# A graph network's scatter sum with weights and stream exchanged in its second round

## The reference, cut to what matters

```python
row, col = edge_index            # = src, dst: 400000 edges, 12500 nodes, H = 64
for t in range(2):               # two rounds
    m_input = concatenate([x[col], x[row], edge_attr], axis=1)
    messages = m_input @ msg_W[t].T + msg_b[t]
    agg = segment_sum(messages, row, num_segments=12500)
    x = gru_cell(agg, x, ...)    # r, z = sigmoid(...), n = tanh(...), (1 - z) * n + z * x
```

## Time and profile before

| | us |
|---|---|
| median of 3 runs | 2404.67 |
| lowest, highest | 2390.03, 2408.36 |
| the profiled execution | 2394.16 |
| its span, first to last instruction | 2392.5 |
| first tile of round 2 to the end, about | 1568 to 2392 |

### The profile page before, as it was taken

How to read it: one execution, slowest core, us unless ns; L and a number is a source line. 1 busy time by engine, 2 the same in 40 slices (tenths; PEclk the granted TensorE clock), 3 DMA queues, 4 the chain that set the end, 5 groups by cost and what they waited for, 6 DMA issues and landing times. The chain is left out here.

```text
span 2392.5 us, 126600 instructions
## 1 busy us (share of the span) xinstructions
PE 1623.6 (68%) x47260; PEld 1526.9 (64%) x47260; DVE 2179.6 (91%) x3727; ACT 1963.7 (82%) x4428; POOL 616.3 (26%) x853
## 2 busy tenths in 40 slices
PE   0000000000139999999999999869999999999996
PEld 0000000000138899999999999868999999999996
DVE  7999999999269899999999999868999999999995
ACT  4777894553158899999999999868999999999996
POOL 1000000000643344554444544301121211112121
PEclk9999999999969999999999999989999999999998
DMA  6100001111427676666677676566777777777773
GB/s 118 28 0 0 0 0 48 35 22 34 113 57 239 211 227 226 227 229 223 231 224 231 226 229 227 167 200 218 236 239 231 237 241 232 235 239 234 234 237 113
DMA packets 175418, 400.70 MB, mean 167 GB/s; under 512 B 73071, under 2 KB 76789, under 8 KB 174855
## 3 DMA queue, kind: packets, MB, share of 16 engines
q1 hardware_dynamic: 116907, 204.17, 27.6%
q0 software_dynamic: 57296, 195.19, 24.7%
q10 hardware_dynamic: 1132, 0.27, 0.1%
HBM read 384.63 MB, written 14.57 MB: 167 GB/s over the span
## 5 line engine op out<-in xcount | busy, mean ns | idle before, releaser
L1202 ACT ACTIVATE rows<-ps_rows 128x512 f16<-128x512 f32 x2744 | 1454.6, 632 | 74.7 <-PE ps_rows L1124 55.5
L1141 PE MATMUL ps_sum<-rows,src 128*64 128x132 f16 (+1 forms) x21952 | 1151.5, 225 | 16.0 <-ACT rows L1202 11.0
L1141 PEld LDWEIGHTS ps_sum<-rows,src 128*64 128x64 f16 x21952 | 903.0, 142 | 29.0 <-ACT rows L1202 20.1
L1296 DVE TENSOR_TENSOR src<-iota_units,src_lane 128x2048 f16<-128x2048 f16 (+1 forms) x784 | 863.4, 1101 | 41.7 <-PE ps_sum L1141 41.6
L1124 PE MATMUL ps_rows<-rows_next,dst 128*64 128x128 f16 x10976 | 546.3, 220 | 37.9 <-DVE dst L1287 21.0
L1124 PE MATMUL ps_rows<-rows_now,dst 128*64 128x128 f16 x10976 | 545.4, 219 | 18.2 <-DVE dst L1287 7.3
L1287 DVE TENSOR_SCALAR dst<-lanes,lane_no 128x2048 f16<-128x2048 f16 (+1 forms) x784 | 533.0, 680 | 10.4 <-DMA lanes<-lanes_dram 10.1
L860 PE MATMUL ps_src<-ident,late 112*64 112x112 f32 x98 | 29.6, 333 | 624.6 <-DVE taken L930 613.0
L1124 PEld LDWEIGHTS ps_rows<-rows_next,dst 128*64 128x64 f16 x10976 | 411.3, 112 | 60.2 <-ACT rows L1202 21.5
L1124 PEld LDWEIGHTS ps_rows<-rows_now,dst 128*64 128x64 f16 x10976 | 412.0, 111 | 41.7 <-issue 12.7
L860 PEld LDWEIGHTS ps_src<-ident,late 112*64 112x64 f32 x98 | 14.1, 143 | 630.2 <-DVE taken L930 614.1
(11 more groups left out here) (188 smaller groups left out, 2039.0 us busy)
## 6 DMA issues: line engine op xcount, KB each, us to landing
lanes<-lanes_dram POOLq DMA_DIRECT2D x294, 512.0 KB, 4.9
lanes<-lanes_dram SPq DMA_DIRECT2D x294, 512.0 KB, 4.7
lanes<-lanes_dram POOLq DMA_DIRECT2D x98, 256.0 KB, 4.2
lanes<-lanes_dram SPq DMA_DIRECT2D x98, 256.0 KB, 4.2
rows_now<-parts_dram SPq DMA_DIRECT2D x112, 32.0 KB, 1.8
rows_next<-parts_dram SPq DMA_DIRECT2D x112, 32.0 KB, 3.8
parts_dram<-rows_now SPq DMA_DIRECT2D x1, 3136.0 KB, 16.2
sorted_dram<-planes SPq DMA_DIRECT2D x1, 3136.0 KB, 11.6
```

Of the source, the lines that this page charges most:

```text
L1141: last = nc.tensor.matmul(ps_sum[b][at, 0:width], hot[:, at], row, start=(j == 0), stop=(j == J - 1))
L1202: nc.scalar.activation(rows[:, (u + NU * b) % ring, 0:n, 0:2 * H], cut(ps_rows[(u + NU * b) % 4][:])[:, 0:n, :], ACT.Copy).then_inc(rows_r ...
L1296: nc.vector.tensor_tensor(src1[q][:, 0:len(units)], iota_units[:].rearrange("p (o l) k -> p o l k", o=1) .broadcast_to([P, len(units), P, ...
```

## The change

Only round 2 (`flipped = r > 0`) changes, and some preparation for it.

1. **Scatter.** Weights are now `row[:, at]`, 64 columns without gaps (once the high, once the low half), and the stream is `hot`, all 128 one-hot columns with their step of 8 bytes. The number of matmuls is the same. `ps_sum` then holds the sums already turned: high half in partitions 0 to 63, low half in 64 to 127.
2. **Taking the sums.** ScalarE's `take_sum` is gone. VectorE writes `scaled`, then low half / 2048 from PSUM into `sums` (64 x 128), then adds the high half from PSUM straight into `turned_now` (64 x 128). `joined` and the copy to `extras` are gone.
3. **Turning.** Only `copied` and `scaled` are turned: two matmuls for four; ScalarE copies 128 columns for 256.
4. **Extras.** Attribute sums and counts of all tiles are turned once, in tile 0, copied by ScalarE, stored to `extras_dram` by SyncE, and for every tile SyncE fetches 2 x 128 numbers into `turned_now`, behind a wait for the gates of two tiles before. SyncE does not go on to tile 1's lanes before the store has landed.
5. **Weights.** As the operands' places are exchanged in round 2, 13 transfers place the weights instead of 8.
6. **The end.** The last two tiles are turned ahead of the last scatter units instead of behind them.

```diff
-                sp.wait_ge(weights_in, 16 * 8)
+                sp.wait_ge(weights_in, 16 * 13)
...
+                    def fetch_extras(k, b):
+
+                        wait(sp, gates_ready, k - 1)
+                        plain(sp.dma_start(turned_now[b][H + 1:H + 3, P:2 * P],
+                                           extras_dram[bass.ds(k, 1), :, :].rearrange("o v p -> (o v) p"))).then_inc(extras_in[b], 16)
+
                     if not more:
                         def body(s, b, half):
                             fetch_lanes(sp, s)
+                            if not past(s, 1):
+                                sp.wait_ge(extras_kept, 1)
+                                sp.dma_start(extras_dram.rearrange("t v p -> t (v p)"), extras_across[0:NT, :]).then_inc(extras_out, 16)
+                                sp.wait_ge(extras_out, 16)
+                                sp.wait_ge(ones_in, 4)
+                            else:
+                                fetch_extras(s - 1, 1 - b)
...
                         if u == 0:
-                            wait(te, sum_ready, s - 1)
+                            wait(te, joined_ready if flipped else sum_ready, s - 1)
...
                             for at in HALVES:
-                                last = nc.tensor.matmul(ps_sum[b][at, 0:width], hot[:, at], row,
-                                                        start=(j == 0), stop=(j == J - 1))
+                                if flipped:
+                                    last = nc.tensor.matmul(ps_sum[b][at, 0:P], row[:, at], hot, start=(j == 0), stop=(j == J - 1))
+                                else:
+                                    last = nc.tensor.matmul(ps_sum[b][at, 0:width], hot[:, at], row,
+                                                            start=(j == 0), stop=(j == J - 1))
...
+                        if flipped:
+                            te.wait_ge(extras_kept, 1)
+                            nc.tensor.matmul(ps_T[high, 0:P], copied[b][:], ident[:], start=True, stop=True)
+                            nc.tensor.matmul(ps_T[low, 0:P], scaled[b][:], ident[:], start=True, stop=True).then_inc(turned, 1)
+                            return
...
+                        if flipped:
+                            te.wait_ge(joined_ready, k + 1)
+                            te.wait_ge(extras_in[b], 16 * half + 16)
...
+                    def turn_extras():
+                        for v in range(2):
+                            last = nc.tensor.transpose(ps_T[0:NT, v * P:(v + 1) * P], edge_sums[:, :, v], ident[:])
+                        last.then_inc(extras_turned, 1)
...
                     def take_sum(k, b):
+                        if flipped:
+                            return
...
+                        n = P if flipped else 2 * P
+                        nc.scalar.activation(turned_now[b][:, 0:n], ps_T[:, 0:n], ACT.Copy).then_inc(T_ready, 1)
...
+                        if flipped:
+                            wait(dve, turned, k - 1)
+                            plain(nc.vector.tensor_scalar(scaled[b][:], h[:, bass.ds(k, 1), 0:H].rearrange("p o f -> p (o f)"),
+                                                          both[:, 1:2], None, ALU.mult)).then_inc(scaled_ready, 1)
+                            dve.wait_ge(scattered, (k + 1) * NU)
+                            wait(dve, joined_ready, k - 1)
+                            nc.vector.tensor_scalar(sums[b][:], ps_sum[b][P - H:P, 0:P], 1.0 / LO, None, ALU.mult).then_inc(sum_ready, 1)
+                            dve.wait_ge(sum_ready, k + 1)
+                            wait(dve, gates_ready, k - 1)
+                            nc.vector.tensor_tensor(turned_now[b][0:H, P:2 * P], sums[b][:], ps_sum[b][0:H, 0:P],
+                                                    ALU.add).then_inc(joined_ready, 1)
+                            return
```

More of the change, by code:

```diff
@@ L970, in sums_round @@
         def sums_round(r, scope):
-            copied, extras, scaled, turned_now = [[sb(f"{name}{b}", [P, n], scope=scope) for b in range(2)] for name, n in
-                                          (("copied", H), ("extras", H), ("scaled", H), ("turned_now", 2 * P))]
+            copied, scaled, turned_now = [[sb(f"{name}{b}", [P, n], scope=scope) for b in range(2)] for name, n in
+                                          (("copied", H), ("scaled", H), ("turned_now", 2 * P))]
+            if r == 0:
+                extras = [sb(f"extras{b}", [P, H], scope=scope) for b in range(2)]
+            else:
+                extras_across = sb("extras_across", [P, 2 * P], scope=scope)
             rz, tn, cand = [sb(name, [P, 2, n], scope=scope) for name, n in (("rz", 2 * H), ("tn", H), ("cand", H))]
@@ L980, in sums_round @@
             more = r + 1 < ROUNDS
+            flipped = r > 0
             ring = NU if r == 0 else 4
@@ L1178, in body @@
                             gather(s, u, b)
+                            if flipped and not later_tile and u == TURN_AT:
+                                turn_extras()
                             if u >= LAG:
@@ L1189, in _ @@
                     for u in range(NU - LAG, NU):
+                        if flipped and u < NU - LAG + 2:
+                            turn(NT - 2 + u - NU + LAG, u - NU + LAG)
                         scatter(NT - 1, u, (NT - 1) % 2)
                     for k in range(NT - 2, NT):
-                        turn(k, k % 2)
+                        if not flipped:
+                            turn(k, k % 2)
                         gates(k, k % 2, k // 2)
@@ L1249, in body @@
                             take(s, u, b)
+                            if flipped and not one_back and u == TURN_AT + 1:
+                                take_extras()
                             if one_back and u == SUM_AT:
@@ L1267, in _ @@
                         take_low(last - 2)
-                    take_sum(NT - 1, b)
+                    if not flipped:
+                        take_sum(NT - 1, b)
                     take_turned(NT - 2, 1 - b)
                     take_turned(NT - 1, b)
+                    if flipped:
+                        take_sum(NT - 1, b)
                     tanhs(last - 1)
```

63 lines of the change are left out of this document (45 added, 18 removed).

## The result

The changed kernel takes 2653.57 us, the median of 6 runs (2649.17 to 2657.69), against 2400.15 for the kernel before in the same comparison (6 runs, 2390.03 to 2408.36): ratio 1.106, 95% interval 1.103 to 1.109. It is slower by 253 us. The execution that was profiled took 2654.41, its span 2652.9; that of before 2394.16 and 2392.5.

What follows compares the result with a forecast made beforehand. TensorE was taken to bound the kernel, with VectorE close behind. Profiled time 2394 + 291 (scatter) - 21 (turning) - 12 (loop branch) + 1 (weights) - 1 (end) = 2652 us; range 2385 to 2700.

Steps and rivals of the forecast that it cites:

- The scatter: Round 2's scatter on TensorE: stream at 8-byte step reads at half speed, 53 ns more per pair, +291 us.
- The forecast group of 0.45: Sign in TensorE's timeline: scatter groups 0.45 us from start to start would show the half-speed stream.
- the loop's branch: Round 2's loop: part of the 0.52 us lost per pass hides behind longer TensorE groups, taken as -12 us.
- Turning: TensorE's turning in each tile: two of four matmul pairs go, 0.215 us per tile, -21 us.
- VectorE: VectorE's three steps for a tile's sums: 0.69 us, 16.05 per pass, no cost while TensorE's pass is longer.
- Extras: SyncE's new waits in the loop and at round 2's start: price 0, upper bound at the start +4 us.
- Weights: Five more weight transfers on SyncE's queue ahead of the window loads: 0 to +3 us, taken as +1.
- One: Round 2's scatter stream keeps its pace and VectorE ends the pass: 2393 us, chance 0.32.
- Two: Stream keeps its pace, but lanes come late or engines wait for each other: 2443 us, chance 0.03.
- three: Stream keeps its pace, VectorE's steps are cheap and TensorE stays the bound: 2346 us, chance 0.04.
- Four: Scatter's two side-by-side streams share one half-speed reader: 217 ns per pair, +875 us, 3250 us, chance 0.04.

Runs made afterwards that it cites:

- e1: Changed kernel, round 2's stream read without gaps instead of at a step of 8 bytes (wrong one-hots): 2393.27 us, ratio to before 0.998.
- e2: Changed kernel, round 2's stream read at a step of 4 bytes instead of 8 (wrong one-hots): 2391.62 us, ratio to before 0.996.
- e3: Changed kernel, round 2's stream read at a step of 16 bytes, across two units (wrong one-hots): 3267.72 us, one run.
- e6: Changed kernel with src's one-hots laid out in twos, 4 bytes apart, in both rounds, same function: 2393.09 us, ratio to before 0.996.
- e4: Kernel before, round 2's scatter weights read without gaps instead of at a step of 8 bytes (wrong one-hots): 2385.29 us, ratio 0.993.
- e5: Kernel before with src's one-hots laid out in twos, 4 bytes apart, in both rounds, same function: 2381.99 us, ratio 0.992.

## Why the prediction was right

**The scatter.** Predicted 53 ns for a pair, +291 us; measured 56 ns, which over 5488 pairs is 306. The step of the argument that carried it was to read the price of a stepped stream, which no row had, from stepped weight loads; the changed kernel shows the same pace in the stream (111 / 128 = 0.87 ns for a column, as in the loads), and e1, e2 and e3 that the distance in bytes decides. Whether one and the same reader serves both is not shown. The float32 loads that the prediction leaned on as well (L860, L861) lie in a stretch with a mean granted clock of 0.68, so that only their shortest could be compared; the argument stands without them. The forecast group of 0.45 was 0.44 to 0.45. Two terms beside it made up for the 15 us: the loop's branch gave back 0.52 us for a pass, -23, where I took half; and the first 14 tiles lost 32 us and not 38, because before is slow there for other reasons. So the mechanism was right, and that the whole meets the forecast to 2 us (260 for 258 between the profiled executions) is luck: the errors of its terms cancel.

**Turning.** Predicted -0.215 us for a tile; measured 0.43 - 0.24 = 0.19, -19 us in place of -21.

**VectorE.** Predicted 0.69 us for its three steps and 16.05 for a pass if it ends the pass. The steps take 0.82, since `sums` is held up behind `scaled` (0.29 from start to start, where I had 0.16): as a term of its own it was 0.13 too small. Even so the pass alone is 15.83, where these steps would make it 15.41 + 2 x 0.45 = 16.31. Half of the missing 0.48 us is in the last quarter's comparison, in one of the two tiles of a pass:

```profile
1808.20 0.93 DVE L1296 TENSOR_TENSOR src<-iota_units,src_lane 128x1024 f16<-128x1024 f16 x1
```

It takes 0.93 us in the kernel before and 0.68 in the kernels where VectorE ends the pass. That fits a short wait for the scatter that the profile counts into the instruction, but is only argued. The rest is spread: from start to start the wait for the scatter was 0.77 us and not 0.69, and two other comparisons took 0.05 and 0.06 longer. So VectorE's own work in the kernel before was 15.83 - 0.90 = 14.9 us of a pass and not 15.41. As long as TensorE's pass took 21.48 us none of this mattered.

**Extras.** Taken as 0, bound +4. In the loop SyncE's waits delay nothing: VectorE never waits for lanes there. At the start the second wait of 3.5 us is there; moving it is worth at most 3 us of a profiled stretch.

**Weights.** Taken as +1, bound +3; measured 2.6, 0.6 of it by the mechanism I gave.

**The rivals.** One was wrong in its condition and right in its consequence: e1 and e6 are that case, with VectorE at the end of the pass, and take 2393.27 and 2393.09 us against 2393 worked out. The agreement is luck in part: VectorE's pass is 15.83 us and not 16.05, and of the 12 us that this gives over 44 passes round 2 shows 5 (824.9 to 819.6). Two and three need a stream at full pace, and the change as made hasn't one; with such a stream (e6) lanes are not late in the loop and VectorE is not cheap. Four, one reader for the two streams side by side, falls with the group of 0.44.

## What to carry over

Look at the distance in bytes between the numbers that TensorE takes in, in the weights as in the stream: at 4 bytes both are at full pace or within 0.01 us for a group of it, at 8 at half. A stepped operand is cheaper as the weights, where its 64 columns can hide behind 128 of stream, than as the stream, where nothing hides it; and before exchanging the two, ask which of them has the step. If the engine that writes the operand does not mind, as VectorE did not here, change the layout: it took five statements and made either kernel faster.

## What the runs showed that I had not expected

- Time at a step stops growing at 16 bytes: 57, 111, 223 and 227 ns for a pair at 4, 8, 16 and 32 bytes.
- A read that "just fits" is not free: 56 ns of slow weight load inside a pair of 57.5 cost the kernel before 0.02 us for a group, 12.5 us where it was taken away in round 2 (e4) and 20.9 where it was in both rounds (e5).
- The time that a loop's branch costs TensorE, 0.52 us for a pass, vanished as its matmuls became longer: both tiles of a pass take 10.74 us.
- A loop of 112 DMA issues took up to 2.0 us longer in one family of kernels than in the other, with the same code; its cause stays open.
